# Routed feed-forward stage: slots of 128 rows taken in pairs, one expert for each half

## The reference, cut to what matters

```python
xf = layernorm(x, ln2_w).reshape(4096, 256)
probs = softmax(xf @ router_w)                 # 8 experts
rw, sel = top_k(probs, 2); rw = rw / rw.sum(-1)
h = gelu(einsum('nc,ecf->enf', xf, w1e), approximate=False)   # F = 512
y_all = einsum('enf,efc->nec', h, w2e)
y = (take_along_axis(y_all, sel) * rw).sum(axis=1)
```

## Time and profile before

| | us |
|---|---|
| runs | 3570.03, 3558.45, 3560.76 |
| median | 3560.76 |
| profiled execution, its own time | 3572.31 |
| its span (first to last instruction) | 3570.6 |
| mean granted TensorE clock, share of full speed | 0.902 |

### The profile page before, as it was taken

How to read it: one execution, slowest core, us unless ns; L and a number is a source line. 1 busy time by engine, 2 the same in 40 slices (tenths; PEclk the granted TensorE clock), 3 DMA queues, 4 the chain that set the end, 5 groups by cost and what they waited for, 6 DMA issues and landing times. The chain is left out here.

```text
span 3570.6 us, 71359 instructions
## 1 busy us (share of the span) xinstructions
PE 2932.0 (82%) x26488; PEld 1934.9 (54%) x26488; DVE 2005.1 (56%) x4626; ACT 1671.8 (47%) x3110; POOL 880.7 (25%) x820
## 2 busy tenths in 40 slices
PE   5888675888779999999879987999209968999993
PEld 3544353444446666666545545666208955666671
DVE  4777454777655444433367765776714334555546
ACT  3767332666534444444357663666315523333331
POOL 5332005555100000000222214331260024333312
PEclk8999896999969999999889997999559978999995
DMA  3221002111124000000011111110142324333211
GB/s 110 68 66 56 13 1 74 59 61 59 35 61 150 1 1 1 1 1 1 22 57 50 58 35 37 39 47 30 45 156 90 93 85 88 73 81 78 70 25 47
DMA packets 195048, 189.58 MB, mean 53 GB/s; under 512 B 25925, under 2 KB 173273, under 8 KB 194553
## 3 DMA queue, kind: packets, MB, share of 16 engines
q1 hardware_dynamic: 188568, 168.24, 15.5%
q0 software_dynamic: 6144, 16.79, 1.6%
HBM read 66.70 MB, written 41.42 MB: 30 GB/s over the span
## 5 line engine op out<-in xcount | busy, mean ns | idle before, releaser
L1481 DVE TENSOR_TENSOR f1H<-f1HF,f1H 128x512 bf16<-128x512 f32 x256 | 176.7, 692 | 397.7 <-ACT f1H L1326 397.7
L1259 PE MATMUL ps<-f1xT,f1w 128*128 128x512 bf16 x1536 | 379.9, 384 | 5.9 <-ACT f1H L1326 5.9
L1281 PE MATMUL ps<-f1w,f1H 128*128 128x256 bf16 x3072 | 379.1, 274 | 0.0
L1281 PEld LDWEIGHTS ps<-f1w,f1H 128*128 128x128 bf16 x3072 | 301.9, 98 | 90.9 <-issue 1.7
L1323 ACT ACTIVATE f1HF<-ps 128x512 f32<-128x512 f32 x256 | 152.8, 597 | 335.2 <-PE ps L1259 335.1
L1259 PEld LDWEIGHTS ps<-f1xT,f1w 128*128 128x128 bf16 x1536 | 148.5, 99 | 152.5 <-issue 18.8
L801 DVE TENSOR_REDUCE a0NM<-ps 128x2 f32<-128x512 f32 x256 | 166.7, 685 | 65.6 <-PE ps L500 65.4
L801 DVE TENSOR_REDUCE a1NM<-ps 128x2 f32<-128x512 f32 x256 | 166.4, 686 | 49.5 <-PE ps L500 46.8
L801 DVE TENSOR_REDUCE a2NM<-ps 128x2 f32<-128x512 f32 x256 | 166.0, 686 | 26.8 <-PE ps L500 25.2
L798 DVE TENSOR_REDUCE a3NM<-ps 128x1 f32<-128x128 f32 (+1 forms) x512 | 149.6, 350 | 42.6 <-PE ps L522 39.3
L684 ACT ACTIVATE a1PT<-ps 128x512 f32<-128x512 f32 x256 | 144.3, 595 | 53.0 <-PE ps L511 51.4
(11 more groups left out here) (566 smaller groups left out, 7150.6 us busy)
## 6 DMA issues: line engine op xcount, KB each, us to landing
a4KS<-a4KH SPq DMA_DIRECT2D x96, 128.0 KB
a4QS<-a4QH SPq DMA_DIRECT2D x96, 128.0 KB, 2.6
slots<-zeros SPq DMA_DIRECT2D x1, 9984.0 KB, 31.5
f2XS<-slots SPq DMA_DIRECT2D x39, 256.0 KB
results<-f2XS SPq DMA_DIRECT2D x39, 256.0 KB, 2.1
f1WF<-in_f_w SPq DMA_DIRECT2D x32, 256.0 KB, 2.7
f2WF<-in_f_w SPq DMA_DIRECT2D x16, 512.0 KB, 5.1
a0KS<-a0KH SPq DMA_DIRECT2D x96, 64.0 KB
```

The source lines that it names most:

```text
L1259: m = nc.tensor.matmul(ps[:, (u * NCH + i) % 2, :], w1[:, x, kt, i * P:i * P + P], xT[:, half, y, kt, :], start=(j == 0), stop=(j == len(t ...
L1281: m = nc.tensor.matmul(out, H[:, (u * NCH + i) % HR, x, t * P:t * P + P], w2[:, y, i, :], start=first, stop=(f == YC - 1 and j == 2 and no ...
L1481: nc.vector.tensor_tensor(H[:, (u * NCH + i) % HR, 1, :], HF[:, (u * NCH + i) % 2, :], H[:, (u * NCH + i) % HR, 0, :], SUB).then_inc(S["h_ ...
```

## The change

Slots have 128 rows, and there are 2*4096/128 + 8 = 72 of them. They are handled in 36 pairs. A turn still takes 256 rows; the first 128 belong to the expert of slot 2j, the other 128 to that of slot 2j+1. So a turn loads two expert numbers, `up` has two matmuls of 128 columns where it had one of 256, and `down` takes the expert of each half.

```diff
-SLOT = 256
+SLOT = 128
 EXPERTS = 8
-SLOT_TILES = 2 * TOK // SLOT + EXPERTS - 1
+SLOT_TILES = 2 * TOK // SLOT + EXPERTS
+PAIRS = SLOT_TILES // 2
...
-                for j in range(SLOT_TILES + R3):
-                    if j < SLOT_TILES:
+                for j in range(PAIRS + R3):
+                    if j < PAIRS:
                         sp.wait_ge(S["e_T"].sem, S["e_T"].at(j - R3, 1))
-                        sp.dma_start(XG[:, j % R3], slots[j * SLOT:(j + 1) * SLOT, :].rearrange("(s p) c -> p s c", p=P)
+                        sp.dma_start(XG[:, j % R3], slots[j * 2 * SLOT:(j + 1) * 2 * SLOT, :].rearrange("(s p) c -> p s c", p=P)
...
                 def up(j):
-                    e = expert[j]
...
                             todo = [(x, y, kt) for kt in range(KT) for x, y in ((0, 0), (0, 1), (1, 0))]
-                            for i, (x, y, kt) in enumerate(todo):
-                                w = w1e[:, x, kt, bass.ds(e, 1), f * P:f * P + P].rearrange("p e c -> p (e c)")
-                                m = nc.tensor.matmul(ps[:, 2 * (j % 2) + half, c * 256:c * 256 + 256], w,
-                                                     eT[:, j % 2, y, kt, :], start=(i == 0), stop=(i == len(todo) - 1))
+                            for s_ in range(2):
+                                e = expert[2 * j + s_]
+                                out = ps[:, 2 * (j % 2) + half, c * 256 + s_ * P:c * 256 + s_ * P + P]
+                                for i, (x, y, kt) in enumerate(todo):
+                                    w = w1e[:, x, kt, bass.ds(e, 1), f * P:f * P + P].rearrange("p e c -> p (e c)")
+                                    m = nc.tensor.matmul(out, w, eT[:, j % 2, y, kt, s_ * P:s_ * P + P],
+                                                         start=(i == 0), stop=(i == len(todo) - 1))
...
                 def down(j):
-                    e = expert[j]
...
                     for s_ in range(2):
+                        e = expert[2 * j + s_]
                         todo = [(x, y, f) for f in range(FC) for x, y in ((0, 0), (0, 1), (1, 0))]
...
-                expert[0] = pe.value_load(EI[0:1, 0:1], min_val=0, max_val=E - 1)
+                for k in range(2):
+                    expert[k] = pe.value_load(EI[0:1, k:k + 1], min_val=0, max_val=E - 1)
                 turn(0)
-                for j in range(SLOT_TILES + 1):
-                    if j + 1 < SLOT_TILES:
-                        expert[j + 1] = pe.value_load(EI[0:1, j + 1:j + 2], min_val=0, max_val=E - 1)
+                for j in range(PAIRS + 1):
+                    if j + 1 < PAIRS:
+                        for k in range(2 * j + 2, 2 * j + 4):
+                            expert[k] = pe.value_load(EI[0:1, k:k + 1], min_val=0, max_val=E - 1)
                         turn(j + 1)
...
-                link(nc.vector.tensor_scalar(CI[:], CI[:], 8, 8, ALU.arith_shift_right, ALU.logical_shift_left))
+                link(nc.vector.tensor_scalar(CI[:], CI[:], 7, 7, ALU.arith_shift_right, ALU.logical_shift_left))
```

More of the change, by code:

```diff
@@ L445, in _ @@
                                 kept_ = S["e_kept%d" % r]
-                                pool.wait_ge(kept_.sem, kept_.at((SLOT_TILES - 1 - r) // 3, 1))
+                                pool.wait_ge(kept_.sem, kept_.at((PAIRS - 1 - r) // 3, 1))
                         pool.wait_ge(S["x_joined"].sem, S["x_joined"].at(u - 2, 1))
@@ L1146, in _ @@
                                  g["zeros"][:].rearrange("p (one c) -> p one c", one=1
-                                                         ).to_broadcast([P, 2 * SLOT_TILES, 2 * D])
+                                                         ).to_broadcast([P, SLOT_TILES * SLOT // P, 2 * D])
                                  ).then_inc(S["r_zero"].sem, 16)
@@ L1593, in _ @@
                         sp.wait_ge(S["e_out"].sem, S["e_out"].at(k, 1))
-                        sp.dma_start(results[k * SLOT:(k + 1) * SLOT, :].rearrange("(s p) c -> p s c", p=P),
+                        sp.dma_start(results[k * 2 * SLOT:(k + 1) * 2 * SLOT, :].rearrange("(s p) c -> p s c", p=P),
                                      OB[:, k % R3].rearrange("p (s c) -> p s c", s=2)
@@ L1742, in _ @@
                 copied(0)
-                for j in range(SLOT_TILES):
-                    if j + 1 < SLOT_TILES:
+                for j in range(PAIRS):
+                    if j + 1 < PAIRS:
                         copied(j + 1)
```

## The result

| | us |
|---|---|
| changed kernel, median of 6 runs | 3625.97 (3623.63 to 3631.79) |
| before, median of 6 runs beside it | 3562.39 (3555.35 to 3570.38) |
| ratio | 1.018, 95% interval 1.0162 to 1.0198 |
| profiled execution: its time, its span | 3626.30, 3624.4 |

The change makes the kernel 64 us slower. The forecast was 3616, +55.6 us, in a range of 3588 to 3634.

What follows compares the result with a forecast made beforehand. PE's array bounds the kernel at 5.68 us a turn; changed, its sequencer would at 7.70. So 36 x 7.70 = 277.2 us against 221.6, +55.6 us: 3616 us, range 3588 to 3634.

Steps and rivals of the forecast that it cites:

- What bounds the kernel before: Expert loop: PE's array bounds at 5.68 us a turn; PE's sequencer is near at 4.3 us, 1.4 us of cover.
- Counts: Register instructions in the loop: 48 addresses a turn in place of 24; 1152 for `up`, 576 for `down`, 72 expert loads.
- The array's own turn, 5.75 us: PE's array in a changed turn: `up` 2.69, `down` 2.62, transposes 0.45 us, together 5.75.
- The sequencer's turn, 7.70 us: PE's sequencer in a changed turn: addresses 5.95, load to first address 1.0, second load 0.65, wait 0.1 us; sum 7.70.
- The block of two loads, wait and transposes' issue: Sequencer's turn: 1.0 us from load to first address plus 0.65 for a second load, together 1.65.
- The step of 124 ns: Sequencer time from one address instruction to the next, matmul issue included, read where it runs freely: 7 steps in about 0.87 us.
- a few late fetches: Sequencer's turn, upper bound: with hand-over times read at 0.1 us, these may raise a turn to 8.1 us.
- the loop's fill and drain: Start and end of the expert loop: claimed to stay about 4 us.
- What was costed at nothing: Sequencer waits, SP's loads and stores, the larger expert table on DVE, first expert loads, zeroing DMA, later layers: no added time.
- the clock rival: PE's clock falls because waiting makes holes; one turn in ten at half clock adds 14 us: 3630 us; chance 0.05.
- The array rival: Loop stays array-bound at 5.75 us a turn, addresses hidden: 14.6 us less, 3546.2 us; chance 0.08.
- Weights: Weight loads bound `up` at 98 ns a matmul, total 3619 us, or 81 ns, total 3590; chance 0.06 for either.

Runs made afterwards that it cites:

- run with more loads: Kernel before, 39 turns, with each turn's load of the expert number done four times: 3593.20 us in one run, against 3568.80 of before.
- the run that lets nothing else bind: Changed kernel, but each turn loads one expert number and uses it for both halves: 3557.71 us against 3568.80 of before, ratio 0.9967.
- pairs in `down` only: Changed kernel, but `up` uses the first half's expert for all 256 rows in 24 matmuls of 256 columns: 3555.97 us against 3568.80 of before, ratio 0.9968.
- the run with two of three products: Changed kernel with one of three products of each piece left out, same addresses and loads: 3622.60 us in one run, against 3560.38 of before.

## Why the prediction was right, point by point

*What bounds the kernel before.* PE's array, with the sequencer near it: right. The run with more loads found its spare time at 1.2 us for a turn, where the prediction had 1.4.

*Counts.* 48 addresses and 2 loads for a turn, 1152, 576 and 72 in all: right to the number (70 of the loads are on the line shown, 2 ahead of the loop).

*The array's own turn, 5.75 us:* 5.76 in the run that lets nothing else bind.

*The sequencer's turn, 7.70 us:* it is 8.0, and this is the mis-sized term. The block of two loads, wait and transposes' issue was put at 1.65 and is 1.5. The addresses were put at 48 x 0.124 = 5.95, and take from 2782.4 to 2786.7 and from 2786.8 to 2788.9, 6.4 us, so 0.133 each. The step of 124 ns is there, but it is the shortest and commonest, not the mean. Two windows of 0.88 us in one turn's `up`, the first free, the second with a long step in it:

```profile
L1686 PEldq FUSED_REGOPS  x8: 46/46/46, 2782.8 to 2783.7; - x8
...
L1686 PEldq FUSED_REGOPS  x6: 46/46/46, 2783.6 to 2784.4; - x6
```

The prediction took its step from a free stretch of less than a microsecond, where no long step happened to fall. The later one now and then was named ("a few late fetches") only in the upper bound. 36 x 0.3 us is 11 us more than forecast; the loop grew by 62.4 where 55.6 were forecast, 7 more. The other 4 us are what the loop's fill and drain are shorter: 288.0 is just 36 x 8.0, while 225.6 is 39 x 5.68 and 4.0, and the prediction had left those 4 us standing. So the forecast's total is nearer than its turn: the two errors, 11 us and 4, partly cancel, which is luck.

*What was costed at nothing.* SP, DVE, ACT and the waits: right, in that the sequencer's turn has no hole and PE waits in it for "issue" alone. The clock stayed at 1.00.

*A misreading.* The prediction says that slices with PE busy at 7 or 8 tenths show clock 8 or 9. Two of the four slices at 7 show 6 and 7. So these rows speak less against the clock rival than the prediction has it; the changed kernel's clock of 1.00 in the loop is what rules it out.

*Rivals.* The array rival needed addresses of at most 83 ns or 32 of them. With 32 (pairs in `down` only) the kernel was indeed faster than before, though its turn of 5.88 us is still the sequencer's. Weights: refuted. Clock: did not occur. The change does do what it says: the tile rows fall from 39 x 256 to 36 x 256. With 24 addresses and one load a turn (same expert for both halves) that brought 11 us by the medians, 6 to 17 by the interval, where 15 were worked out.

*What stays open.* Where the longer steps come from. They are some 30 to 170 ns above 124 and come back in the sequencer's queue every microsecond or so. The records of the changed kernel and of the run with two of three products tell two kinds apart. The usual one comes 8 addresses after the last in both kernels, although 32 instructions pass in the one and 24 in the other, so it does not follow the count of instructions. The largest, 260 ns and more from address to address, come nearly always 52 to 60 addresses apart in the changed kernel and mostly 68 to 76, or twice that, in the other; with 217 and 169 instructions for 48 addresses, both are about 250 instructions. With 24 fewer matmuls and 24 fewer weight loads in a turn the turn lost 0.06 us. What the sequencer does in these steps was not measured, and no run isolates it.

## What to carry to other kernels

In this kernel an operand indexed by a run-time value costs PE's sequencer one register instruction for each distinct address. Count those and multiply by the step between them over a whole turn (0.13 us here), not by the 46 ns of the record, then compare with the array's time for the matmuls between. Cutting a matmul in two with two different dynamic weights doubles that count while the columns stay the same. Where only a few units of work can be mixed, lay the data out so that their number is bounded at build time, and spread them: the spare time of the turns before and after takes up nearly half of what each adds, and the sequencer's lead some of the rest.

## What the runs showed of the hardware that I had not expected

A stream of 48 matmuls of 128 columns, each with its own weight load of 98 ns, ran at 56 ns a matmul, equal to the transposes. And a pair among turns of one expert, which adds 3.8 us of sequencer work (24 addresses and a load), costs only 0.5 to 0.9 us: most of it falls into spare time, and the 32 addresses of its `up` started 0.8 to 1.4 us ahead of their matmuls.
